# Attention and feed-forward kernel on one core: order of score matmuls, a clip in halves, and small jobs dealt to other beats

## What is computed

```python
qkv = x @ w_qkv.T;  k_y = split_heads(x @ w_ky.T)
L   = einsum('bhqd,bhkd->bhqk', q, k)   * scale          # "W scores", for the weights
L_y = einsum('bhqd,bhkd->bhqk', q, k_y) * scale          # "Y scores", for the sum
agg = sum(exp(clip(L_y, -15, 15)) * mask, -1) + EPS
w   = softplus(log(abs(L) + EPS) - log(agg + EPS)) * mask
out = einsum('bhqk,bhkd->bhqd', w / (sum(w, -1) + EPS), v) @ w_proj.T
x   = layernorm(x + out);   x = layernorm(x + ffn(x))
```

## Time and profile before

| | us |
|---|---|
| median of three executions | 1312.37 (1307.35 to 1312.47) |
| the profiled execution | 1316.58 |
| its span, first to last instruction | 1314.8 |
| PE busy | 1193.9 (91%) |
| DVE busy | 733.0 (56%) |
| ACT busy | 657.7 (50%) |
| POOL busy | 198.8 (15%) |

### The profile page before, as it was taken

How to read it: one execution, slowest core, us unless ns; L and a number is a source line. 1 busy time by engine, 2 the same in 40 slices (tenths; PEclk the granted TensorE clock), 3 DMA queues, 4 the chain that set the end, 5 groups by cost and what they waited for, 6 DMA issues and landing times.

```text
span 1314.8 us, 23936 instructions
## 1 busy us (share of the span) xinstructions
PE 1193.9 (91%) x8214; PEld 810.9 (62%) x8214; DVE 733.0 (56%) x1229; ACT 657.7 (50%) x963; POOL 198.8 (15%) x235
## 2 busy tenths in 40 slices
PE   2888888888888899877999999999999999999996
PEld 1444444444444444434888787887878878878785
DVE  1466859697887878675645335244353263433523
ACT  3678878788887878765413214133241241321411
POOL 1333323333333333320000000000000000000000
PEclk9999989999999999987999999999999999999999
DMA  4355656657476655429300000000000000000000
GB/s 142 74 144 134 184 151 184 183 142 216 129 224 157 200 141 166 92 76 345 113 33 17 16 17 32 0 16 32 16 32 0 16 32 16 16 16 16 32 0 17
DMA packets 62527, 117.27 MB, mean 89 GB/s; under 512 B 8976, under 2 KB 14608, under 8 KB 62480
## 3 DMA queue, kind: packets, MB, share of 16 engines
q1 hardware_dynamic: 62480, 116.64, 31.3%
HBM read 46.35 MB, written 19.92 MB: 50 GB/s over the span
## 4 chain that ended last, share of the span: by engine, by line
issue 51%; PE 4%; DVE 2%; POOL 0%; DMA 0%; ACT 0%; POOLq 0%; DVEq 0%; SPq 0%; ACTq 0%
PE score_banks L1160 1%; DVE w_ring L786 1%; PE score_banks L1046 1%; PE acc_bank L1074 0%; PE misc_bank L1140 0%; PE misc_bank L1105 0%; PE misc_bank L1003 0%; DMA qc_stack<-qc_lo 0%; PE misc_bank L1038 0%; POOL f_rstd L1303 0%; DVE stats L1292 0%; DVE base_v L838 0%; DVE f_xt_lo L868 0%; DVE base_v L834 0%; POOL rstd L1303 0%
## 5 line engine op out<-in xcount | busy, mean ns | idle before, releaser
L661 ACT ACTIVATE f_h_full<-score_banks,f_scales 128x512 f32<-128x512 f32 x128 | 88.2, 689 | 358.5 <-PE score_banks L1160 358.4
L786 DVE TENSOR_TENSOR w_ring<-score_banks,keep 128x1024 int32<-128x1024 int32 (+1 forms) x192 | 191.6, 1040 | 31.6 <-PE score_banks L1046 31.5
L1160 PE MATMUL score_banks<-f_ha_hi,f_w_all 128*128 128x512 f32 x512 | 205.2, 401 | 2.9 <-DVE f_h_full L881 2.3
L1160 PE MATMUL score_banks<-f_hb_hi,f_w_all 128*128 128x512 f32 x512 | 203.2, 397 | 0.0
L1160 PE MATMUL score_banks<-f_hb_lo,f_w_all 128*128 128x512 f32 x512 | 201.7, 394 | 0.0
L1160 PE MATMUL score_banks<-f_ha_lo,f_w_all 128*128 128x512 f32 x512 | 201.4, 393 | 0.0
L592 ACT ACTIVATE w_ring<-w_ring 128x1024 f32<-128x1024 f32 (+1 forms) x192 | 176.3, 919 | 34.5 <-DVE w_ring L786 34.0
L585 ACT ACTIVATE e_ring<-score_banks 128x1024 f32<-128x1024 f32 (+1 forms) x192 | 158.1, 876 | 36.5 <-PE score_banks L1046 36.4
L777 DVE TENSOR_SCALAR e_ring<-e_ring 128x2048 f32<-128x2048 f32 (+1 forms) x96 | 101.0, 1052 | 113.6 <-ACT e_ring L585 113.5
L461 POOL TENSOR_SCALAR_AFFINE_SELECT e_ring<-e_ring 128x512 f32<-128x512 f32 (+1 forms) x96 | 78.8, 820 | 317.9 <-DVE e_ring L777 310.9
L1160 PEld LDWEIGHTS score_banks<-f_ha_hi,f_w_all 128*128 128x128 f32 x512 | 96.3, 188 | 34.4 <-DVE f_ha_lo L874 6.6
(11 more groups left out here) (123 smaller groups left out, 1792.5 us busy)
## 6 DMA issues: line engine op xcount, KB each, us to landing
piece<-in_wf SPq DMA_DIRECT2D x44, 256.0 KB, 2.9
wf_copy<-piece SPq DMA_DIRECT2D x44, 256.0 KB, 3.0
ky_stack<-ky_hi SPq DMA_DIRECT2D x64, 128.0 KB, 2.5
ky_stack<-ky_lo SPq DMA_DIRECT2D x64, 128.0 KB, 2.6
k_stack<-k_hi SPq DMA_DIRECT2D x64, 128.0 KB, 2.6
k_stack<-k_lo SPq DMA_DIRECT2D x64, 128.0 KB, 2.6
f_w_all<-wf_copy SPq DMA_DIRECT2D x2, 4096.0 KB, 25.7
f_x_turn<-x SPq DMA_DIRECT2D x9, 512.0 KB, 3.3
```

The lines of the kernel that those rows point to most:

```text
L661: nc.scalar.activation(h_full[m % 2][:], f_bank[m % F_RING], ACT.Gelu, scale=scales[:, 1 + layer, m:m + 1]).then_inc(gelu_done, 1)
L786: nc.vector.tensor_tensor(w_ring[:, t % RING, 2 * i:2 * i + 2, 0:cols].bitcast(I32), pair_banks(w_pair(t, i), cols).bitcast(I32), keep[:, ...
L1160: mm = nc.tensor.matmul(out, left.bitcast(dt), right.bitcast(dt), start=first and n == 0, stop=last and n == 1)
```

## The change

- TensorE, beat 0: `sum_values` is cut in two. Its second half, `sum_prefixes`, now comes after `scores_w`. Beat 3: `q_proj` is cut in two; its second half comes after `scores_w`.
- TensorE and ScalarE: the two `turn`s of the attention output move from beats 0 and 2 to beats 2 and 3.
- VectorE, beats 0 and 3 (`EARLY`): the clip is two instructions of half the size, each after its own half of exps, with the matching half of `absolute` behind each. GpSimd's `mask_e` waits for both.
- VectorE and ScalarE: `split_x` moves from beat 0 of the odd slot to beat 5 of the even slot before it. The pieces are halved and compared in beats 0, 2, 3, 4 instead of 0, 1, 2, 3. `normalise` is cut: its last multiplication goes behind beat 0's `absolute` in the next slot. Half of the layer norm's statistics moves from beat 3 of the odd slot to beat 5 of the even slot.
- ScalarE: `v_sum_keep` comes after the second `logs` in all slots (before: in odd slots only).
- SP: `stack_qc` issues its high part without waiting for the low one; `stack_qc(0)` and `stack_ky` are ahead of `load_piece(2)`, and `stack_qc(1)` and `stack_k` ahead of `load_piece(3)`.

```diff
+CHECK_BEATS = (0, 2, 3, 4)
+EARLY = (0, CHUNKS)
+CLIPS = (2, 3, 4, 6, 7, 8)
...
             def stack_qc(v, g):
+                reach_alone(sp, w_scores, BEATS * (v.index - 1) + CHUNKS * (g + 1), sp_passed)
+                reach_alone(sp, qc_hi_made, v.index + 1, sp_passed)
+                stack(qc_stack[g][:], 0, qc_hi, g, qc_stacked[g])
                 reach_alone(sp, qc_lo_made, v.index + 1, sp_passed)
-                reach_alone(sp, w_scores, BEATS * (v.index - 1) + CHUNKS * (g + 1), sp_passed)
-                stack(qc_stack[g][:], 0, qc_hi, g, qc_stacked[g])
                 stack(qc_stack[g][:], 1, qc_lo, g, qc_stacked[g])
...
-                if check and check != "last":
-                    load_piece(k, 2, check)
                 if 3 in w:
                     stack_qc(k.shift(-1), 0)
                 if project:
                     stack_ky(k.shift(1), 0)
                 if check and check != "last":
-                    load_piece(k, 3, check)
+                    load_piece(k, 2, check)
                 if 3 in w:
                     stack_qc(k.shift(-1), 1)
                     stack_k(k.shift(-1), 1)
+                if check and check != "last":
+                    load_piece(k, 3, check)
...
+            def clip_half(k, t, i):
+                cols = CHUNK_COLS[t % CHUNKS]
+                reach(dve, exp_done, 2 * y_beat(k, t) + i + 1)
+                tiles = e_ring[:, t % E_RING, 2 * i:2 * i + 2, 0:cols]
+                nc.vector.tensor_scalar(tiles, tiles, math.exp(CLIP), math.exp(-CLIP), ALU.min, ALU.max).then_inc(e_clipped, 1)
...
+                    if y and t in w and t in EARLY:
+                        for i in range(2):
+                            clip_half(k, t, i)
+                            absolute(k, t, (i,))
...
+                    if t == 0 and output is not None:
+                        divide_sums(output)
...
+                    if t == 5 and next_x is not None:
+                        split_x(next_x)
+                    if t == 5 and output is not None:
+                        reach(dve, res_made, 2 * output + 1)
+                        norm_rows(nc, output, 0, norm_tiles)
                     if t == 5 and divide is not None and not final:
-                        normalise(divide)
+                        add_base(divide)
...
                     if t == 3 and project:
-                        q_proj(k.shift(1))
+                        q_proj(k.shift(1), (0,))
...
                     if t in w:
                         scores_w(k, t, y)
+                    if t == 0 and 3 in w:
+                        sum_prefixes(k.shift(-1))
+                    if t == 3 and project:
+                        q_proj(k.shift(1), (1,))
...
-                    if t == 0 and output is not None:
-                        turn(output, 0)
...
-                    if t == 2 and output is not None:
-                        turn(output, 1)
+                    if t in (2, 3) and output is not None:
+                        turn(output, t - 2)
```

More of the change, by code:

```diff
@@ L262, in weights_of, with clipped, check_step @@
             return (k.shift(-1), t - CHUNKS) if t >= CHUNKS else (k.shift(-2), t + CHUNKS)
+        def clipped(k, t):
+            return CLIPS[-1] * k.index + CLIPS[t]
+        def check_step(t, check):
+            if not check or t not in CHECK_BEATS:
+                return None
+            s = CHECK_BEATS.index(t)
+            return s if (check != "first" or s > 0) and (check != "last" or s == 0) else None
         def y_pair(t, i):
@@ L707, in slot @@
                         v_keep(k)
[L708 to L709 removed]
                     if t == 1 and project:
                         ky_keep(k.shift(1))
[L712 to L713 removed]
+                    if t in (2, 3) and output is not None:
+                        turn_keep(output, t - 2)
                     if t == 4 and y:
                         k_keep(k)
[L716 to L717 removed]
+                    if check_step(t, check) is not None:
+                        piece_halve(k, check_step(t, check))
                     if t == 0 and any(before):
@@ L784, in absolute @@
                 reach(dve, w_scores, w_beat(k, t) + 1)
-                for i in range(2):
+                for i in pairs:
                     nc.vector.tensor_tensor(w_ring[:, t % RING, 2 * i:2 * i + 2, 0:cols].bitcast(I32),
@@ L823, in normalise, with add_base @@
             def normalise(b):
+                add_base(b)
+                divide_sums(b)
+            def add_base(b):
                 start = ATT_STEPS * b
@@ L953, in slot @@
                         keep_agg(k, 0)
[L954 to L959, removed]
+                    if y and t in w and t in EARLY:
+                        for i in range(2):
+                            clip_half(k, t, i)
+                            absolute(k, t, (i,))
+                    else:
+                        if y and t in EARLY:
+                            for i in range(2):
+                                clip_half(k, t, i)
+                        elif y:
+                            clip(k, t)
+                        if t in w:
+                            absolute(k, t)
+                    if t == 0 and output is not None:
+                        divide_sums(output)
                     if t == 2 and norm is not None:
@@ L1004, in project_t, with project_split @@
                 mm.then_inc(done, 1)
-            def project_split(u, kind, done):
+            def project_split(u, kind, done, kts=range(DT)):
                 m = slice(P * u.half, P * u.half + P)
-                for kt in range(DT):
+                for kt in kts:
                     hi, lo = w_hi[:, kt, kind, m], w_lo[:, kt, kind, m]
@@ L1013, in project_split, with q_proj @@
                     mm = nc.tensor.matmul(misc[:], hi, xq_lo[:, kt, :], start=False, stop=kt == DT - 1)
[L1014 to L1019, removed]
+                if DT - 1 in kts:
+                    mm.then_inc(done, 1)
+            def q_proj(u, kts=range(DT)):
+                if 0 in kts:
+                    take_misc((q_made, u.index + 1))
+                    reach(pe, xq_split, u.batch + 1)
+                project_split(u, 0, q_ready, kts)
             def ky_proj(u):
@@ L1288, in norm_statistics, with norm_rows, norm_aggregate @@
 def norm_statistics(nc, dve, b, s):
+    for half in range(2):
+        norm_rows(nc, b, half, s)
+    norm_aggregate(nc, dve, b, s)
+def norm_rows(nc, b, half, s):
+    for i in range(2 * half, 2 * half + 2):
+        nc.vector.bn_stats(s["stats"][:, i, :], s["res"][:, i, :]).then_inc(s["ln_step"], 1)
+def norm_aggregate(nc, dve, b, s):
     base = LN_STEPS * b
-    for i in range(TI):
-        nc.vector.bn_stats(s["stats"][:, i, :], s["res"][:, i, :]).then_inc(s["ln_step"], 1)
     reach_alone(dve, s["ln_step"], base + TI, s["passed"])
```

42 lines of the change are left out of this document (22 added, 20 removed).

## The result

The changed kernel takes 1302.05 us (median of eight executions, 1299.77 to 1303.79) against 1310.97 us (eight, 1306.44 to 1312.73) for the kernel before: a ratio of 0.9928 with a 95% interval of 0.9912 to 0.9944, 8.9 us less. The forecast was 1299 (1284 to 1311), faster. The profiled execution took 1303.79, with a span of 1301.7.

What follows compares the result with a forecast made beforehand. TensorE, VectorE and ScalarE, 75 to 90% busy, pass work round a ring. Pairs 9.8, late DMAs 0.9 and other slots 2.4 took 13.1 us off 1316.58, giving 1303.5; the median 4.2 lower, so 1299 (8 in 10: 1284 to 1311).

Steps and rivals of the forecast that it cites:

- Odd slot, beat 0: TensorE's whole gap at the AND before scores_y of beat 1 goes: minus 0.9 us; split clip costs VectorE 192 ns.
- Odd slot, beats 1 and 2: split_x leaves and the 0.47 us idle before scores_y of beat 2 goes; that scores_y starts 0.95 us earlier.
- Odd slot, beats 3 and 4: scores_y of beat 4 1.9 us earlier, shrinking to 0.5 on ScalarE, 1.15 at k_proj; new slot 33.7 us, minus 1.1.
- Even slot: Beat 2 gains 1.4 us, beat 3 loses its qc_stack wait but gives it back; 35.6 us against the usual 35.9.
- The sum: Seven steady pairs at 1.4 us (9.8), late DMAs 0.9, slots without norm and drain slots 2.4: together 13.1 us less.
- late DMAs: One to two even slots where scores_w of beat 3 waits for a late qc_stack: 0.9 us gained in all.
- the drain slots: Two drain slots have the beat-0 gap but little behind it: 0.4 us gained each.
- The signs: AND waits under 0.2 us, slots 33.7 and 35.6, acc_copy and att_raw waits about 1 in beat 4, no qc_stack wait, compare 0.68.
- A: Rival: ScalarE gives the gain back as waits for copy_sums, keep_att and exps; gain 0 to 6 us, 1306 to 1312; chance 0.2.
- B: Rival: in beat 3 the cut q_proj puts the ring on a longer path; plus 9 us, 1321; chance 0.08.
- C: Rival: TensorE's gaps go and nothing takes their place; 25 to 38 us less, 1280; chance 0.17.
- D: Rival: split_x meets GpSimd's base_times in even beat 5; 0 to 4 us, 1299 to 1303; inside the forecast's 0.55.

Runs made afterwards that it cites:

- e9: Changed kernel without any cut (sum_values, q_proj and clip whole), small jobs and SP's order kept: 1300.74 us, 0.9904 of the kernel before.
- e10: The changed kernel itself, run again as yardstick: 1300.20 us, 0.9900 of the kernel before.
- e1: Changed kernel with q_proj in one piece again, ahead of scores_w in beat 3: 1293.53 us, 0.9851 of the kernel before.
- e2: Changed kernel with sum_values whole, sum_prefixes back in front of scores_w in beat 0: 1308.85 us, 0.9980 of the kernel before.

## Why the prediction was right

*Odd slot, beat 0.* Minus 0.9 forecast, 0.77 measured. VectorE was 0.7 us late for the first clip, behind split_x and a part of the statistics, without TensorE waiting for it. The split of the clip costs 0.15 us (twice 0.68 or 0.69 less 1.22), not 0.19, which changes nothing.

*Odd slot, beats 1 and 2.* Scores_y of beat 2 at 11.1 after that of beat 0 was forecast (410.5 - 399.41), 11.26 measured (12.03 before).

*Odd slot, beats 3 and 4.* The working said that the 1.9 us, counted from the start of the slot, would shrink to 0.5 on ScalarE's chain and grow again to 1.15 at k_proj. Measured it is 1.8 at scores_y of beat 4, 0.24 at scores_w of beat 4 and 1.07 at k_proj, by the named links: q_keep late, then a wait of 1.0 for copy_sums (1.20 measured) and 0.25 for exps (0.22), and keep_att earlier. Slot 33.7 forecast, 33.82 measured.

*Even slot.* 35.6 forecast, 35.85 measured. Turn's wait for q_keep is 0.69 (forecast 0.75), and the three waits in beat 4 are 0.34, 0.22 and 0.42 (forecast 0.35, 0.3 and 0.55). As against the usual even slot before, nothing was gained: beats 0 and 1 lost 0.14 where nothing was forecast, beat 2 gained 1.30 instead of 1.4, and beats 3 and 4 gave back 1.19 instead of 1.1.

*The sum.* Pair 1.4 forecast, 1.0 measured: the mis-sized term is the even slot, 0.3 forecast, 0.0 measured. Nor were there seven such pairs. The five of batches 2 to 6, apart from late DMAs and clock, gave 4.9 us; the four slots of batches 0 and 1 gave 1.0, the even slot of batch 7 lost 1.0, and the first scores_y came 0.6 later. The stretch from unit (7, 1) on, with the drain slots, gave 2.4 us where 0.8 stood for the drain slots; the granted clock is low in parts of it in both. The even slots with late DMAs gave 0.7 us in batch 6 and some 1.9 in batches 2 and 3, where 0.9 was forecast for all. The remaining 3.8 or so are low clock in the one execution. So it is luck that the sum of 13.1 us equals the 13.1 us between the two spans; the medians differ by 8.9. The distance of the profiled execution from the median was taken off as 4.2; against the median of eight it is 5.6. The forecast of 1299 lies 3 us below what was measured, and within its range.

*The signs.* Most came true: the wait for the AND before scores_y of beats 1 and 4, the odd slot, the wait for copy_sums in beat 4, qc_stack. Two did not. The compare does not take 0.68 us throughout: in even slots two of the compares meet GpSimd's subtractions at their new places (1.10 and 1.45 us), which the forecast left out when it took the compare away from the old one. And TensorE's wait for keep_att in beat 4 did not grow to about 1 us; in the odd slot it fell from 1.18 to 0.34, as the working itself had said against its own sign.

*The rivals.* A, that ScalarE gives it back, was given 0.2. For the cuts more than that happened in the steady slots: they gave back all they had gained and 0.8 us a pair besides (e9 beside e10). For the kernel as a whole it did not, since the jobs pay for themselves. B, that the cut of q_proj costs more than it earns, was given 0.08 as a reason for a slower kernel. Its mechanism is real (e1: 6.3 us between the spans of e1 and e10, 6 to 10 by the ratios), and it took away a third to a half of what the rest had gained. What failed in B was the size of the other side. C did not happen. D's collision is there and nearly doubles split_x:

```profile
354.47 1.99 POOL L497 TENSOR_TENSOR v_before<-v_before,v_aug 128x128 f32<-128x128 f32 x2
...
389.47 1.94 POOL L505 TENSOR_TENSOR base_v<-v_sum,base 128x1024 f32<-128x1024 f32 x1
...
390.25 2.24 DVE L781 TENSOR_TENSOR xq_lo<-xq,xq_hi 128x1024 fp32r<-128x1024 f32 x1
```

The rows are v_before beside add_base, then base_times and split_x: 1.99 instead of 1.00 us, and 2.24 us instead of 1.21. No wait of TensorE came from split_x in the steady odd slot, as the lower end of D's price had it. That add_base would meet v_before was not seen; TensorE waits 0.28 us for it where the cut of sum_prefixes does not hide it (e2). The Trainium skill (GPSIMD Engine Reference, Key points) names the contention on the shared SBUF interfaces; these rows agree in kind. That section gives no size.

What the prediction missed is the question to which part the gain belongs. It credited beat 0 and beat 3 to the cuts, each against the kernel before, and did not work out the jobs and SP's order by themselves. e9 and e10 show what that sum had to find: with the jobs dealt out anew, what is left of the wait for the AND costs less in the steady slots than the chain on ScalarE that the cuts make longer. So the number came out near, with the gain booked to the wrong part of the change, and that too is in part luck.

## What to carry to other kernels

A wait of the busiest engine that disappears from the profile is no gain until the next one in the ring has been counted: here 33.4 us of waiting for the AND became 4.8, and the wait for a copy grew from 1.6 to 14.8 us. If a product is cut so that something else goes between its halves, count who reads the whole of it and what stands behind that reader. And where a queue works in order, a job that is moved to a later beat moves all that stands behind its DMA: order the queue first, then deal out the jobs.

## What the runs showed of the hardware

A VectorE instruction with two SBUF operands beside a GpSimd subtraction or multiplication took about twice as long (split_x 2.24 instead of 1.21 us, the compare 1.38 to 1.46 instead of 0.68). GpSimd suffers as well (v_before 1.99 instead of 1.00 us, base_sum 1.28 instead of 0.29), while add_base, beside v_before, kept its 1.21 us. The end times have a pattern: split_x ended 1.08 us after GpSimd's multiplication, the compare of the earlier trace rows and the two of the changed kernel 0.55 or 0.56 us after the subtraction, and base_sum 0.16 us after split_x, each some 0.13 us less than its own length alone. So each looks as if it had stood until the other was through and had then done its whole work; that reading is an inference from these rows. The half clip took 0.69 us where the whole one takes 1.22.
